# Reordering the prologue of a two-layer cross-attention kernel: loads from two queues, keys before queries, weight preparation moved to later slots

## The chip, the cores and the metric

The kernel runs on one NeuronCore of one Trainium2 chip. The metric is the device time of one launch in microseconds (us), as the median of several runs. The profile is one execution of the same program; its times count from the start of its span.

## What is computed

Four batches. Each has 256 queries (`x`) and 512 context rows (`ctx`), all 256 wide. Everything is kept close to float32: large products are made from a high and a low part of each operand.

```python
# layer 0, per batch
z = layer_norm(x, ln1_w, ln1_b)
q = z @ q_w + q_b;  k = ctx @ k_w + k_b;  v = ctx @ v_w + v_b     # 16 heads of 16
p = softmax(where(mask, q k^T / 4, -max))                          # 256 x 512 for each head
h = (p v) @ cproj_w + cproj_b + x
h = h + gelu(layer_norm(h, ln2_w, ln2_b) @ fc_w + fc_b) @ proj_w + proj_b
# layer 1, per batch
p1 = softmax((h w_q^T)(ctx w_k^T)^T / 16)
out = h + alpha * ((p1 (ctx w_v^T)) w_o^T)
```

## The kernel before, in words

Every engine runs its own program, written out by hand: a `prologue`, then `iteration(0)` to `iteration(3)`, then an `epilogue`. Engines meet only through semaphores, and each queue executes strictly in program order. SP issues nearly all transfers.

**Slots.** The attention of a batch is 16 heads in 4 groups of 4 heads, each group 8 tiles (a head's 128 queries by 512 keys). A slot handles one tile: `max_tile` multiplies `q_stack` by `k_stack` into `s1` (L546), VectorE takes the row maximum (`take_max`, L1284), `split_max` cuts the maxima into three bfloat16 parts, `max_rows` (L553) and `rows` (L977) write them into `q_stack`, `exp_tile` multiplies again, transposed and with the maxima subtracted (L563), ScalarE takes the exponential (L986), and `pv` multiplies by the values (L573). Maxima are one group ahead of exponentials. Slots are numbered 0 to 31 within a batch; iteration `b` runs slots 7 to 31 of batch `b` and 0 to 6 of batch `b+1`, and beside them, at slot numbers from the tables `PRE_AT` and `EARLY_AT`, the projections `pre(b+1, n)` of the next batch. `EARLY_AT` serves batch 1. Iterations 1 to 3 also carry the rest of the layers (`post`) of the batch before, which iteration 0 does not have. In its place iteration 0 prepares late weights: `PREP_AT` (TensorE, ScalarE) and `PREP_LOW_AT` (VectorE) give the slots of the steps WA, WT, CB, WO, WC, WF0, WF1, WP0, WP1 (L816 to L842 on TensorE).

**Stacks.** To reach float32 accuracy in bfloat16 products, a batch's queries `qp` and keys `kp` are cut into three parts (high, middle, low), and `stack_heads(b, c)` copies them, for the 8 heads of half `c`, into `q_stack` and `k_stack`: six transfers of 64 KB for the queries (L419), one mask row (L421), six transfers of 128 KB for the keys (L427). Before the change the queries go first. All 13 must land before half `c`'s first `max_tile`. For a later batch a half may be overwritten only once the exponentials that read it are through:

```python
await_alone(sp, s2_full, NS * (b - 1) + SLOTS * (2 * c + 2))
```

so `stack_heads(1, 0)` starts when slot 15 of batch 0 has been multiplied, and must land before slot 24, whose `max_tile` belongs to batch 1. `stack_heads(1, 1)` starts after slot 31.

**Parts.** The high part is written by ScalarE, the rest `qf - high` by GpSimd (`query_rest`, `key_rest`, L1627, L1635), the middle part by ScalarE, the low part by GpSimd (`query_low`, `key_low`, L1631, L1639). There is one buffer `kf` for both key halves.

**Prologue before.** SP loads `xz` (x of batch 0), `cx` (its context), `raw_q`, six rows of small vectors, two bias rows, `raw_k`, the mask and `raw_v`. TensorE transposes context and normalised x (`pre` with `U_CT`, `U_ZT`), then makes the vector columns (L854), a bias product (L859), turns the two bias rows into columns (L865), then `U_Q` (query product), `U_K`, `U_K+1` (key products), `U_V`, the 8 maxima of group 0, `U_V+1`, `max_rows` and slots 0 to 6. Products wait for low parts of weights that ScalarE and VectorE make. SP then issues the selector rows (L445), `stack_heads(0, 0)`, the loads of batch 1 (`load_pre(1)`: `xz`, mask, `cx`), `stack_heads(0, 1)`, and the late weights (L450 to L456).

The functions that the diff touches, with the line numbers of the profile:

Of the kernel before, what the change touches and what calls it, by code (L numbers as in the profile page):

```python
# [26 lines left out]
F32 = mybir.dt.float32  # L27
# [7 lines left out]
P = 128  # L35
B, LQ, D = 4, 256, 256
LK = 512
# [30 lines left out]

LN1_AT = 7
# [10 lines left out]
EARLY_AT = {7: U_CT, 8: U_CT + 1, 9: U_ZT, 10: U_Q, 14: U_K, 22: U_K + 1}  # L80
# [5 lines left out]
PREP_AT = {8: "WA", 10: "WT", 12: "CB", 13: "WO", 14: "WC", 16: "WF0", 18: "WF1", 24: "WP0", 26: "WP1",  # L86
           38: "END"}
PREP_LOW_AT = {11: "WT", 12: "WA", 13: "CB", 14: "WO", 15: "WC", 22: "WF0", 23: "WF1", 28: "WP1", 30: "WP0"}
# [36 lines left out]
def build(nc, x, ctx, mask, ln1_w, ln1_b, q_w, q_b, k_w, k_b, v_w, v_b, cproj_w, cproj_b, ln2_w, ln2_b,  # L125
          fc_w, fc_b, proj_w, proj_b, l1_q, l1_k, l1_v, l1_o, alpha, out):
    with ExitStack() as stack:
# [31 lines left out]
        bk = sb("bk", [P, DC])  # L159
        bf = sb("bf", [P, FC])  # L160
# [35 lines left out]
        qk_rows = oT[0:1, 0:2, :]  # L196
        qk_perm = oT[0:1, 2:4, :]
# [53 lines left out]
        l1_in, wf_in, wp_in = sem("l1_in"), sem("wf_in"), sem("wp_in")  # L251
# [53 lines left out]

        def pre_bank(b, n):

            if isinstance(b, int) and b == 0:
                return (pre_ps[:], post_ps[:, 0, :], post_ps[:, 1, :])[n % 3]
            return pre_ps[:]  # L310
# [86 lines left out]
        def _(sp):  # L397
# [11 lines left out]
            def stack_heads(b, c):  # L409

                heads = slice(c * HC, (c + 1) * HC)

                await_alone(sp, s2_full, NS * (b - 1) + SLOTS * (2 * c + 2))

                made = ((pre_free, PRE_USES * b + U_Q + 1), (qm_done, b + 1), (q_parts, b + 1))
                for part, (sem_, n) in enumerate(made):
                    await_alone(sp, sem_, n)
                    for i in [i for i, p in enumerate(TERMS_Q) if p == part]:
                        sp.dma_start(q_stack[i * HD:(i + 1) * HD, heads, :], qp[:, part, c, :]).then_inc(stacked[c], 16)  # L419
                await_alone(sp, row_done, b + 1)  # L420
                sp.dma_start(k_stack[ROW_MASK:ROW_MASK + 1, heads, :],  # L421
                             mask_row[0:1, :].unsqueeze(1).to_broadcast([1, HC, LK])).then_inc(stacked[c], 16)
                made = ((kh_done, 2 * b + c + 1), (km_done, 2 * b + c + 1), (k_parts, 2 * b + c + 1))
                for part, (sem_, n) in enumerate(made):
                    await_alone(sp, sem_, n)
                    for i in [i for i, p in enumerate(TERMS_K) if p == part]:
                        sp.dma_start(k_stack[i * HD:(i + 1) * HD, heads, :], kp[:, part, c, :]).then_inc(stacked[c], 16)  # L427

            def prologue():
                sp.dma_start(xz[:], x[0].rearrange("(p t) d -> p t d", t=TQ)).then_inc(x_in, 16)  # L430
                sp.dma_start(cx[:], ctx[0].rearrange("(p k) d -> p k d", k=TK)).then_inc(cx_in, 16)
                sp.dma_start(raw_q, q_w.rearrange("(c p) n -> p c n", p=P)).then_inc(wq_in, 16)
                row = 0
                for v in (ln1_w, ln1_b, v_b, ln2_w, ln2_b, fc_b):
                    n = v.shape[0] // P
                    sp.dma_start(vec_rows[row:row + n, :], v.rearrange("(r p) -> r p", p=P)).then_inc(vec_in, 16)
                    row += n
                for i, v in enumerate((q_b, k_b)):
                    sp.dma_start(qk_rows[:, i, :], v.rearrange("(o n) -> o n", o=1)).then_inc(bias_in, 16)
                sp.dma_start(raw_k, k_w.rearrange("(c p) n -> p c n", p=P)).then_inc(wk_in, 16)  # L440
                sp.dma_start(mask_u[:], mask[0:1, :].partition_broadcast(P)).then_inc(mask_in, 16)
                sp.dma_start(raw_v, v_w.rearrange("(c p) n -> p c n", p=P)).then_inc(wv_in, 16)
# [3 lines left out]
                stack_heads(0, 0)  # L446
                load_pre(1)
                stack_heads(0, 1)
                for t, w in zip(raw_l1, (l1_q, l1_k, l1_v, l1_o)):
                    sp.dma_start(t, w.rearrange("(c p) n -> p c n", p=P)).then_inc(l1_in, 16)  # L450
                sp.dma_start(raw_c, cproj_w.rearrange("(c p) n -> p c n", p=P)).then_inc(wc_in, 16)
# [31 lines left out]
        def _(pe):  # L483
# [25 lines left out]
            def pre(b, n):  # L509

                await_(pe, pre_free, PRE_USES * b + n if not (isinstance(b, int) and b == 0) else
                       n - 2 if n < U_Q else max(n - 2, U_ZT + 1))
# [297 lines left out]
            def prepare(step):  # L810

                if step == "WA":
                    pe.wait_ge(l1_in, 16 * 4)
                    for c in range(DC):
                        for k in range(DC):
                            mm = pe.matmul(post_ps[:, 0, c * D:(c + 1) * D], raw_l1[0][:, k, chunk(c)], raw_l1[1][:, k, :],  # L816
                                           start=k == 0, stop=k == DC - 1)
                    mm.then_inc(prep_ps, 1)
                elif step == "WT":
                    for c in range(DC):  # L820
                        for k in range(DC):
                            mm = pe.transpose(post_ps[:, 1, c * D + k * P:c * D + (k + 1) * P], raw_l1[3][:, k, chunk(c)], ident[:])
# [15 lines left out]
                elif step == "WO":  # L838
                    pe.wait_ge(w_lo, 4)
# [5 lines left out]
                elif step == "END":  # L845
                    pe.wait_ge(prep_done, 2)
                    pe.wait_ge(w_lo, 10)

            def prologue():
                pe.wait_ge(consts, 1)  # L850
                for n in range(U_CT, U_ZT + 1):
                    pre(0, n)
                pe.wait_ge(vec_in, 16 * 6)
                pe.transpose(s2[:, 0, 0:VECS], vec_rows[:], ident[0:VECS, 0:VECS]).then_inc(vec_ps, 1)  # L854

                pe.wait_ge(wq_in, 16)
                pe.wait_ge(vec_done, 2)
                for k in range(DC):
                    mm = pe.matmul(s2[0:1, 1, 0:D], vecs[:, V_LN1B + k:V_LN1B + k + 1], raw_q[:, k, :],  # L859
                                   start=k == 0, stop=k == DC - 1)  # L860
                mm.then_inc(bq_ps, 1)

                pe.wait_ge(bq_done, 2)
                for i in range(2 * DC):
                    mm = pe.matmul(s2[:, 1, D + i:D + i + 1], qk_perm[:, i // DC, chunk(i % DC)], ident[0:1, 0:1],  # L865
                                   start=True, stop=True)
                mm.then_inc(bq_ps, 1)
                pe.wait_ge(w_lo, 1)
                pre(0, U_Q)
                pe.wait_ge(w_lo, 2)  # L870
                pre(0, U_K)
                pre(0, U_K + 1)
                pe.wait_ge(w_lo, 3)
                pre(0, U_V)
                pe.wait_ge(sel_in, 16 * NG)
# [3 lines left out]
                max_rows(0, 0)  # L879
                for s in range(START):  # L880
# [56 lines left out]
        def _(act):  # L937
            def pre(b, n):
                if U_K <= n < U_V:
                    return  # L940
                act.wait_ge(pre_full, PRE_USES * b + n + 1)
# [4 lines left out]
                elif n == U_Q:  # L946
# [3 lines left out]
                    await_(act, q_parts, b)  # L950
                    for c in range(DC):
# [14 lines left out]
            def key_high(b, c):  # L966
                await_(act, stacked[c], 16 * STACK_DMAS * b)
                act.wait_ge(pre_free, PRE_USES * b + U_K + c + 1)
# [171 lines left out]
            def prepare(step):  # L1140
                if step == "WA":
                    act.wait_ge(prep_ps, 1)
                    act.activation(wa[0][:].rearrange("p c n -> p (c n)"), post_ps[:, 0, :], ACT.Copy, scale=L1_SCALE)\
                       .then_inc(w_hi, 1)
                elif step == "WO":
                    act.wait_ge(prep_ps, 4)
# [14 lines left out]
            def prologue():  # L1161
                for n in range(U_CT, U_ZT + 1):
                    pre(0, n)

# [5 lines left out]
                act.wait_ge(wk_in, 16)  # L1170
                for k in range(DC):
                    a = act.activation(parts_of(wk[0][:, k, :]), by_head(raw_k[:, k, :]), ACT.Copy)
# [604 lines left out]
```

## Time and profile before

| | |
|---|---|
| median of 3 runs | 336.18 us (334.94 to 336.44) |
| profiled execution, its own time | 335.6 us |
| its span | 333.8 us |
| TensorE matmul busy | 276.5 us, 83% |
| VectorE busy | 218.8 us, 66% |
| ScalarE busy | 189.9 us, 57% |
| GpSimd busy | 90.4 us, 27% |
| mean granted TensorE clock | 0.938 |
| moved by transfers | 21.59 MB |

In the rows below, PE is TensorE, PEld its weight load, DVE VectorE, ACT ScalarE, POOL GpSimd, SPq the issue of a transfer on SP. L numbers are lines of the kernel before. Busy shares are means over stages that have different limits, so the stage that changes has to be read by itself.

### The profile page before, as it was taken

To read this page: it belongs to the slowest core of one execution; us is meant where nothing else is said; L and a number is where in the kernel's file an instruction comes from. 1 tells how busy PE (TensorE), PEld (TensorE's weight loads), DVE (VectorE), ACT (ScalarE), POOL (GpSimd) and SP (SyncE) were. 2 spreads that over 40 slices of the span, in tenths; PEclk is the share of its full clock that TensorE was granted. 3 is DMA by queue.
4 is the path that set the end of the run, shared out by engine and by line. 5 is a ranking of instruction groups with operands and counts; after the bars stand their busy time and mean duration, and the time that the engine had idled before them with its cause. 6 is when DMAs were issued, how large, how long until landed. Compare 5 with 4: busy or idle time off the path is not lost.

```text
span 333.8 us, 5436 instructions
## 1 busy us (share of the span) xinstructions
PE 276.5 (83%) x2065; PEld 199.4 (60%) x2065; DVE 218.8 (66%) x430; ACT 189.9 (57%) x352; POOL 90.4 (27%) x87
## 2 busy tenths in 40 slices
PE   3670978987779897999898979998989997859895
PEld 3460426853226575866585758665956776658784
DVE  4550787377485967886758778867378664454854
ACT  3542084369565569596645695966466697315612
POOL 2143000212200138742002387440010354033300
PEclk9995599779589999999999999999999999978999
DMA  5129996007418202900443029004530000000000
GB/s 186 24 59 138 169 264 211 2 21 115 111 31 112 97 0 66 178 5 0 95 50 128 1 57 119 3 0 93 54 127 0 2 2 0 2 1 0 2 31 31
DMA packets 21489, 21.59 MB, mean 65 GB/s; under 512 B 2388, under 2 KB 18856, under 8 KB 21464
## 3 DMA queue, kind: packets, MB, share of 16 engines
q1 hardware_dynamic: 20168, 18.11, 28.8%
q10 hardware_dynamic: 1296, 3.15, 2.6%
q8 instruction: 16, 0.26, 0.3%
q14 instruction: 9, 0.07, 0.1%
HBM read 10.50 MB, written 1.05 MB: 35 GB/s over the span
## 4 chain that ended last, share of the span: by engine, by line
PE 46%; DVE 24%; ACT 12%; issue 5%; DMA 5%; SPq 4%; POOL 4%; ACTq 0%; DVEq 0%
DVE neg_max L1284 8%; PE post_ps L501 8%; PE om L573 6%; PE pre_ps L488 6%; PE s L546 5%; PE post_ps L505 4%; PE s L563 4%; DMA k_stack<-kp 3%; SPq L419 2%; ACT q_stack L977 2%; SPq L427 2%; PE s L501 2%; DVE ft L1367 1%; ACT probs L986 1%; PE post_ps L835 1%
## 5 line engine op out<-in xcount | busy, mean ns | idle before, releaser
L1284 DVE TENSOR_REDUCE neg_max<-s 128x1 f32<-128x512 f32 x128 | 83.4, 683 | 26.7 <-PE s L546 25.8
L986 ACT ACTIVATE probs<-s 128x512 f32<-128x512 f32 x128 | 75.5, 599 | 28.0 <-PE s L563 27.5
L546 PE MATMUL s<-k_stack,q_stack 97*128 97x512 bf16 x128 | 49.7, 414 | 21.5 <-DMA k_stack<-kp 14.9
L563 PE MATMUL s<-q_stack,k_stack 109*128 109x256 bf16 x256 | 50.6, 281 | 2.5 <-ACT q_stack L977 1.7
L546 PEld LDWEIGHTS s<-k_stack,q_stack 97*128 97x128 bf16 x128 | 12.4, 99 | 47.2 <-DVE neg_max L1284 21.8
L573 PE MATMUL om<-probs,vals 128*17 128x256 f32 x512 | 35.4, 397 | 0.0
L563 PEld LDWEIGHTS s<-q_stack,k_stack 109*128 109x128 bf16 x256 | 20.9, 101 | 16.6 <-ACT q_stack L977 3.6
L1615 POOL TENSOR_TENSOR ln<-ln,minus_half 128x2 f32<-128x2 f32 x8 | 5.6, 703 | 86.9 <-DVE ln L1248 86.9
L977 ACT ACTIVATE q_stack<-om 13x1024 bf16<-13x1024 bf16 x16 | 16.3, 1017 | 13.7 <-PE om L553 13.3
L573 PEld LDWEIGHTS om<-probs,vals 128*17 128x17 f32 x512 | 12.1, 99 | 14.0 <-issue 7.3
L1310 DVE TENSOR_TENSOR y_l<-post_ps,y_h 128x512 fp32r<-128x512 f32 x12 | 8.3, 689 | 16.3 <-ACT y_h L1000 16.3
L1367 DVE SCALAR_TENSOR_TENSOR ft<-ft,fx 128x512 f32<-128x512 f32 x9 | 12.0, 1331 | 7.2 <-POOL ft L1670 7.2
L1000 ACT ACTIVATE y_h<-post_ps 128x512 fp32r<-128x512 f32 x12 | 7.0, 595 | 17.0 <-PE post_ps L505 13.7
L1675 POOL TENSOR_TENSOR y_l<-fx,y_h 128x512 fp32r<-128x512 f32 x9 | 11.5, 1282 | 14.9 <-ACT y_h L1039 14.9
L501 PE MATMUL post_ps<-aT_h,wf_h 128*128 128x256 f32 x48 | 13.7, 319 | 0.0
L501 PE MATMUL post_ps<-wp_h,y_h 128*128 128x256 f32 x48 | 13.6, 314 | 0.0
L1670 POOL TENSOR_TENSOR ft<-fx 128x512 f32<-128x512 f32 x9 | 9.4, 1041 | 15.7 <-ACT fx L1013 15.7
L1635 POOL TENSOR_TENSOR kf<-kf,kp 128x512 f32<-128x512 f32 x8 | 9.3, 1161 | 15.2 <-ACT kp L969 15.2
L1657 POOL TENSOR_TENSOR h<-h,cb 128x512 f32<-128x512 f32 x3 | 3.8, 1271 | 32.2 <-DMA h<-in_x_dram 32.2
L1639 POOL TENSOR_TENSOR kp<-kf,kp 128x512 bf16<-128x512 f32 x8 | 10.2, 1272 | 7.0 <-ACT kp L973 7.0
L501 PE MATMUL post_ps<-wp_l,y_h 128*128 128x256 f32 x48 | 12.0, 283 | 0.0
L501 PE MATMUL post_ps<-aT_h,wf_l 128*128 128x256 f32 x48 | 12.0, 282 | 0.0
(315 smaller groups left out, 715.1 us busy)
## 6 DMA issues: line engine op xcount, KB each, us to landing
k_stack<-kp SPq DMA_DIRECT2D x48, 128.0 KB
q_stack<-qp SPq DMA_DIRECT2D x48, 64.0 KB
cx<-in_ctx_dram SPq DMA_DIRECT2D x4, 512.0 KB, 6.0
pcx<-in_ctx_dram ACTq DMA_DIRECT2D x3, 512.0 KB, 3.6
xz<-in_x_dram SPq DMA_DIRECT2D x5, 256.0 KB, 5.7
raw_late<-in_L_xattn_fc_w_dram SPq DMA_DIRECT2D x1, 1024.0 KB, 12.3
raw_late<-in_L_xattn_proj_w_dram SPq DMA_DIRECT2D x1, 1024.0 KB, 12.1
h<-in_x_dram ACTq DMA_DIRECT2D x3, 256.0 KB, 2.6
```

The lines of the kernel that those rows point to most:

```text
L488: mm = pe.matmul(o, wi(w[a], k), vi(v[c], k), start=start and k == 0 and i == 0, stop=stop and k == n - 1 and i == 2)
L501: pe.matmul(o, wi(w[a], k), vi(v[c], k), start=start and i == k == a == c == 0, stop=False)
L505: mm = pe.matmul(o, wi(w[late[0]], k), vi(v[late[1]], k), start=False, stop=stop and i == len(terms) - 1 and k == n - 1)
L546: pe.matmul(s1[:, s % 2, :], q_stack[0:ROW_MAX, hd, chunk(t)], k_stack[0:ROW_MAX, hd, :], start=True, stop=True).then_inc(s1_full, 1)
L563: mm = pe.matmul(s2[:, s % 2, i * LQ:(i + 1) * LQ], k_stack[:, hd, chunk(k)], q_stack[:, hd, :], start=True, stop=True)
L573: mm = pe.matmul(om[32 * j:32 * j + VW, 0:LQ], vals[:, k, g * GH + j, :], probs[:, g % 2, j, k, :], start=k == 0, stop=k == TK - 1)
L977: act.activation(q_stack[ROW_MASK:ROWS, g * GH:(g + 1) * GH, :], om_rows[ROW_MASK:ROWS, :].unsqueeze(1).to_broadcast([ROWS - ROW_MASK, GH, ...
L986: act.activation(probs[:, g % 2, s // 2, k:k + 2, :], s2[:, s % 2, :].rearrange("p (k n) -> p k n", k=2), ACT.Exp).then_inc(s2_free, 1)
L1284: dve.tensor_reduce(neg_max[:, g % 2, s % 2, s // 2:s // 2 + 1], s1[:, s % 2, :], AX.X, ALU.max, negate=True).then_inc(s1_free, 1)
L1367: dve.scalar_tensor_tensor(f, f, 1.0 / GELU_CUBIC, fx[i % 3], ALU.add, ALU.mult).then_inc(cube, 1)
L1639: pool.tensor_tensor(kp[:, 2, c, :], kf[:], kp[:, 1, c, :], ALU.subtract).then_inc(k_parts, 1)
L1675: pool.tensor_tensor(lo, fx[i % 3], hi.bitcast(F32), ALU.subtract).then_inc(y_split, 1)
```

## The change

SP and ScalarE both issue the first loads. The bias rows are no longer turned into columns by TensorE: four transfers write them as columns of 4-byte elements (`bk`, `qb`). The first key product stands ahead of the query product (`FIRST_ORDER`); the high part of the key weights is made by VectorE, its low part by GpSimd. The parts of the queries and of the first key half are cut on VectorE in place of GpSimd. `stack_heads(0, 0)` copies keys first. WA moves from iteration 0 into the prologue; the other preparation steps move to slots 16 and later. Selector rows, three late weights and `stack_heads(0, 1)` are reordered around the loads of batch 1, and `q_stack`'s memset is cut in two.

```diff
+FIRST_ORDER = (U_CT, U_CT + 1, U_ZT, U_K, U_Q, U_K + 1, U_V, U_V + 1)
-EARLY_AT = {7: U_CT, 8: U_CT + 1, 9: U_ZT, 10: U_Q, 14: U_K, 22: U_K + 1}
+EARLY_AT = {7: 0, 8: 1, 9: 2, 11: 3, 14: 4, 22: 5}
-PREP_AT = {8: "WA", 10: "WT", 12: "CB", 13: "WO", 14: "WC", 16: "WF0", 18: "WF1", 24: "WP0", 26: "WP1", 38: "END"}
-PREP_LOW_AT = {11: "WT", 12: "WA", 13: "CB", 14: "WO", 15: "WC", 22: "WF0", 23: "WF1", 28: "WP1", 30: "WP0"}
+PREP_AT = {16: "WT", 18: "WO", 19: "WC", 21: "CB", 22: "WF0", 24: "WF1", 28: "WP0", 30: "WP1", 38: "END"}
+PREP_LOW_AT = {17: "WT", 19: "WO", 21: "WC", 22: "CB", 24: "WF0", 26: "WF1", 31: "WP0", 36: "WP1"}

 # SP, stack_heads
+                if b == 0 and c == 0:
+                    keys()
+                    queries()
+                else:
+                    queries()
+                    keys()
 # SP, prologue, after xz and cx
-                (raw_q, six vector rows, two bias rows, raw_k, mask_u, raw_v, in this order)
+                for dst, v in ((bk, k_b), (qb, q_b)):
+                    for c in range(DC):
+                        sp.dma_start(dst[:, c:c + 1], v[chunk(c)].rearrange("(h d) -> d h", h=HC).unsqueeze(2),
+                                     allow_slow_non_contiguous=True).then_inc(bias_in, 16)
+                for i, w in ((0, l1_q), (1, l1_k)):
+                    sp.dma_start(raw_l1[i], w.rearrange("(p c) n -> p c n", c=DC)).then_inc(wa_in, 16)
+                stack_heads(0, 0)
                 sp.wait_ge(consts, 2)
                 for g in range(NG):
                     sp.dma_start(k_stack[ROW_MAX:ROWS, g * GH:(g + 1) * GH, :], sel[:]).then_inc(sel_in, 16)
-                stack_heads(0, 0)
+                for i, w in ((2, l1_v), (3, l1_o)):
+                    sp.dma_start(raw_l1[i], w.rearrange("(c p) n -> p c n", p=P)).then_inc(wo_in, 16)
+                sp.dma_start(raw_c, cproj_w.rearrange("(c p) n -> p c n", p=P)).then_inc(wc_in, 16)
+                stack_heads(0, 1)
                 load_pre(1)
-                stack_heads(0, 1)
-                (the four l1 weights and raw_c)
                 (raw_f, cb, pb, alpha_c, raw_p as before)
 # TensorE, prologue
+                vec_rows transposed first, then U_CT, U_CT + 1, U_ZT
+                bias product (4 matmuls of 128 columns), pre(0, U_K),
+                2 one-column matmuls for the bias product alone, pre(0, U_Q), pre(0, U_K + 1),
+                prepare("WA"), pre(0, U_V), 8 max_tile, pre(0, U_V + 1), max_rows
+                pe.wait_ge(sel_in, 16 * NG)      # now after max_rows, was ahead of the first max_tile
 # ScalarE, prologue
+                issues six vector rows, raw_k, raw_q, mask_u, raw_v; then
+                pre(0, U_CT); wq high; pre(0, U_CT + 1); pre(0, U_ZT); qk_row copy; wv high;
+                key_high(0, 0); key_middle(0, 0); pre(0, U_Q); query_middle(0); sel;
+                key_high(0, 1); key_middle(0, 1); prepare("WA"); pre(0, U_V); rows(0, 0); ...
 # VectorE, prologue
+                memset of half of q_stack; norm_stats; vecs; lnq; norm_apply; wk high; lows of U_CT, U_CT + 1;
+                wq low; low of U_ZT; take_mask; pre(0, U_K); bq (2 steps); key_rest(0, 0); wv low;
+                key_low(0, 0); query_rest(0); memset om; query_low(0); memset of the other half of q_stack;
+                pre(0, U_K + 1); memset vals; 8 take_max; split_max; prepare("WA")
 # GpSimd, prologue
+                wk low; mask_row_of(0); h; key_rest(0, 1); key_low(0, 1)
```

Lines with a sign and no code in them give in words the order that the new code has.

## Rows read from the trace of the kernel before

**Rows 1.** The chain that ended last, in order of time, prologue (start, length, what):

```profile
15.13 2.88 PE pre_ps L488 x12
...
27.56 5.73 DMA k_stack<-kp
```

**Rows 2.** SP's issues in order of time (start, length, engine, line, operation, tiles, count):

```profile
13.87 3.19 SPq L445 DMA_DIRECT2D k_stack<-fx  x4
...
24.37 3.79 SPq L427 DMA_DIRECT2D k_stack<-kp  x6
28.20 0.59 SPq L401 DMA_DIRECT2D xz<-in_x_dram  x1
...
72.34 3.77 SPq L419 DMA_DIRECT2D q_stack<-qp  x6
...
76.90 3.79 SPq L427 DMA_DIRECT2D k_stack<-kp  x6
```

**Rows 3.** The same chain in iteration 0:

```profile
51.97 1.73 PE post_ps L816 x8
...
57.89 0.44 PE post_ps L822 x4
...
60.30 0.86 PE post_ps L830 x4
61.16 4.46 PE post_ps L835 x32
...
66.49 3.41 PE post_ps L842 x8
...
80.09 5.74 DMA k_stack<-kp
```

**Rows 4.** Busy us by stretch: length, PE, PEld, DVE, ACT, POOL; granted clock, DMA share, GB/s:

```profile
52.00:72.30 20.30, 20.30 (x135) 15.90 (x134) 10.67 (x20) 8.60 (x18) 2.89 (x3) 0.83 0.17 52
72.30:81.50 9.20, 7.71 (x64) 3.38 (x62) 6.93 (x15) 8.39 (x15) 2.33 (x2) 1.00 0.55 98
...
96.20:110.10 13.90, 12.30 (x94) 7.18 (x92) 8.50 (x21) 8.46 (x15) 0.69 (x1) 0.88 0.58 87
28.00:30.00 2.00, 0.00 (x0) 0.00 (x0) 0.00 (x0) 1.11 (x2) 1.26 (x2) 0.50 1.16 119
32.00:34.00 2.00, 0.57 (x2) 0.14 (x2) 0.00 (x0) 0.00 (x0) 0.00 (x0) 0.50 1.02 268
...
98.00:100.00 2.00, 2.00 (x15) 0.73 (x19) 1.24 (x2) 0.73 (x2) 0.00 (x0) 0.50 0.32 83
```

**Rows 5.** The same view, one stretch inside the step CB:

```profile
61.00:62.00 1.00, 1.00 (x11) 1.00 (x9) 0.02 (x1) 0.00 (x0) 0.30 (x1) 1.00 0.00 0
```

**Rows 6.** Timeline (start, length, engine, line, operation, tiles, count, idle time before), prologue:

```profile
6.84 1.06 PE L517 MATMUL post_ps<-ident,xz 128*128 128x128 f32 x4
...
9.70 1.86 PE L859 MATMUL s<-probs,vecs 128*1 128x256 f32 x4 [1.57 <-DVE lnq L1431]
...
18.82 0.84 ACT L954 ACTIVATE qp<-pre_ps,bq 128x256 bf16<-128x256 f32 x2
...
20.14 0.75 DVE L1279 SCALAR_TENSOR_TENSOR kf<-post_ps,bk,mask_f 128x512 f32<-128x512 f32 x1
...
20.81 0.68 DVE L1383 TENSOR_TENSOR wv_l<-probs,wv_h 128x512 fp32r<-128x512 f32 x1
...
23.97 0.63 ACT L973 ACTIVATE kp<-kf 128x512 bf16<-128x512 f32 x1 [1.88 <-POOL kf L1635]
...
24.68 1.15 POOL L1639 TENSOR_TENSOR kp<-kf,kp 128x512 bf16<-128x512 f32 x1 [0.74 <-ACT kp L973]
```

**Rows 7.** Timeline, iteration 0: batch 1's first context transposes; a low part of weights:

```profile
48.16 0.61 PE L522 MATMUL pre_ps<-ident,cx 128*128 128x128 f32 x4
...
83.00 1.28 DVE L1408 SCALAR_TENSOR_TENSOR wf_l<-raw_late,vecs,wf_h 128x1024 fp32r<-128x1024 f32 x1
```

**Rows 8.** The page's DMA queues: packets, MB, share of 16 engines:

```profile
q1 hardware_dynamic: 20168, 18.11, 28.8%
```

More of the change, by code:

```diff
@@ L304, in bank_of, with pre_place, pre_use @@
             return POST_BANK[n]
+        def pre_place(b, n):
+            return FIRST_ORDER.index(n) if b == 0 else n
+        def pre_use(b, n):
+            return PRE_USES * b + pre_place(b, n) + 1
         def pre_bank(b, n):
-            if isinstance(b, int) and b == 0:
-                return (pre_ps[:], post_ps[:, 0, :], post_ps[:, 1, :])[n % 3]
+            if b == 0:
+                return (pre_ps[:], post_ps[:, 0, :], post_ps[:, 1, :])[pre_place(b, n) % 3]
             return pre_ps[:]
@@ L413, in stack_heads @@
                 await_alone(sp, s2_full, NS * (b - 1) + SLOTS * (2 * c + 2))
[L415 to L427, printed above, removed]
+                def queries():
+                    made = ((pre_free, pre_use(b, U_Q)), (qm_done, b + 1), (q_parts, b + 1))
+                    for part, (sem_, n) in enumerate(made):
+                        await_alone(sp, sem_, n)
+                        for i in [i for i, p in enumerate(TERMS_Q) if p == part]:
+                            sp.dma_start(q_stack[i * HD:(i + 1) * HD, heads, :], qp[:, part, c, :]).then_inc(stacked[c], 16)
@@ new lines, in keys @@
+                def keys():
+                    await_alone(sp, row_done, b + 1)
+                    sp.dma_start(k_stack[ROW_MASK:ROW_MASK + 1, heads, :],
+                                 mask_row[0:1, :].unsqueeze(1).to_broadcast([1, HC, LK])).then_inc(stacked[c], 16)
+                    made = ((kh_done, 2 * b + c + 1), (km_done, 2 * b + c + 1), (k_parts, 2 * b + c + 1))
+                    for part, (sem_, n) in enumerate(made):
+                        await_alone(sp, sem_, n)
+                        for i in [i for i, p in enumerate(TERMS_K) if p == part]:
+                            sp.dma_start(k_stack[i * HD:(i + 1) * HD, heads, :], kp[:, part, c, :]).then_inc(stacked[c], 16)
@@ L509, in pre @@
             def pre(b, n):
-                await_(pe, pre_free, PRE_USES * b + n if not (isinstance(b, int) and b == 0) else
-                       n - 2 if n < U_Q else max(n - 2, U_ZT + 1))
+                at = pre_place(b, n)
+                await_(pe, pre_free, PRE_USES * b + n if b > 0 else max(at - 2, DC if n == U_K else U_ZT + 1) if n > U_ZT else at - 2)
                 if n == U_ZT:
@@ L1161, in prologue @@
             def prologue():
-                for n in range(U_CT, U_ZT + 1):
-                    pre(0, n)
+                row = 0
+                for v in (ln1_w, ln1_b, v_b, ln2_w, ln2_b, fc_b):
+                    n = v.shape[0] // P
+                    act.dma_start(vec_rows[row:row + n, :], v.rearrange("(r p) -> r p", p=P)).then_inc(vec_in, 16)
+                    row += n
+                act.dma_start(raw_k, k_w.rearrange("(c p) n -> p c n", p=P)).then_inc(wk_in, 16)
+                act.dma_start(raw_q, q_w.rearrange("(c p) n -> p c n", p=P)).then_inc(wq_in, 16)
+                act.dma_start(mask_u[:], mask[0:1, :].partition_broadcast(P)).then_inc(mask_in, 16)
+                act.dma_start(raw_v, v_w.rearrange("(c p) n -> p c n", p=P)).then_inc(wv_in, 16)
+                pre(0, U_CT)
                 act.wait_ge(wq_in, 16)
@@ L1701, in prologue @@
                 rstd(ln1, ln1_step, 0, rstd1)
+                pool.wait_ge(wk_hi, 1)
+                for k in range(DC):
+                    i = pool.tensor_tensor(parts_of(wk[1][:, k, :]), by_head(raw_k[:, k, :]),
+                                           parts_of(wk[0][:, k, :]).bitcast(F32), ALU.subtract)
+                i.then_inc(wk_lo, 1)
+                mask_row_of(0)
                 pool.wait_ge(vec_done, 1)
@@ L1705, in prologue @@
                     .then_inc(prep_step, 1)
-                mask_row_of(0)
-                query_rest(0)
-                query_low(0)
-                for c in range(DC):
-                    key_rest(0, c)
-                    key_low(0, c)
+                key_rest(0, 1)
+                key_low(0, 1)
             def tail(step):
```

180 lines of the change are left out of this document (94 added, 86 removed).

## The prediction, made before the changed kernel ran

> **What bounds the kernel now.** I read the page first (busy shares, the 40 slices), then the chain that ended last in order of time, then SP's issues, the timelines and the busy time by stretch. TensorE is busy 83% of the span, and the chain goes through the same steps in iterations 1 and 2. The change does not touch them, so it can only move their start. The stage that matters is the prologue with iteration 0.
>
> In the prologue the chain ends in a transfer: the last key transfer is issued at 27.56 and lands at 33.29 [rows 1], and only then can the first `max_tile` run. SP's six key issues start at 24.37, so the keys take 8.92 us from first issue to landing; for batch 1 they take 76.90 to 85.83, 8.93 us [rows 2, 3]. That is the transfer engines at their limit, not SP: while keys move, the DMA share is 1.16 at 119 GB/s. While queries move it is 0.32 at 83 GB/s, paced by the issues. Loads from memory reach 268 GB/s [rows 4]. The queries stand ahead of the keys, so the slow part starts last.
>
> In iteration 0 the chain is TensorE. From 51.97 to 72.3 it is busy all 20.3 us [rows 4], and five preparation pieces stand in it: 1.73 + 0.44 + 0.86 + 4.46 + 3.41 = 10.9 us [rows 3]. Then slot 15 frees `stack_heads(1, 0)`, which runs from 72.34 [rows 2] to 85.83 [rows 3], 13.5 us. The work of slots 16 to 23 needs only 9.2 us of it [rows 4]; TensorE then waits. So there are two delays in series: the first stacks, and 10.9 us of preparation ahead of a transfer chain that has 4.3 us to spare.
>
> **Step 1, the first stacks.** TensorE finishes the transposes of x at 7.9 [rows 6], as now: the vector transpose ahead of them is short and x and the context come by the same two issues. The bias product costs 1.86 [rows 6], to 9.8. The key weights' low part on GpSimd must be there by then: two instructions of 256 columns, together about the 1.15 us of one of 512 columns [rows 6], after a VectorE copy that I bound by 0.68 [rows 6]. That ends near 9, so it is hidden; if the columns come strided and both double, it is 1 us late. The first key product is six matmuls of 512 columns, as much as twelve of 256, which took 2.88 with their tail [rows 1]; I take 2.7, to 12.5. VectorE evicts in 0.75, ScalarE makes the high part in 0.63 [rows 6]: first key issue at 14.0 in place of 24.37. The middle and low parts (0.68 on VectorE, 0.63, 0.68 [rows 6]) are ready before SP, at 0.63 an issue, wants them. Keys land at 14.0 + 8.9 = 22.9.
>
> The queries now come behind. Their product ends at about 15.7, two times 0.84 on ScalarE [rows 6] takes it to 17.3, and rest, middle, low (0.68 + 0.63 + 0.68) to 19.4, so SP's twelve issues run from 14.0 to 21.6 with almost no hole. The 384 KB of queries wait behind the keys and must drain after 22.9. Their own limit is not in the trace. At the loads' 268 GB/s they take 1.4 us; at the keys' 119 they take 3.2; if they pass beside the keys, nothing. Queries at 0.32 share were far from saturated, so I take the first end, 1.3: stacks at 24.2, **9.1 us earlier** than 33.29 (bounds 7.1 and 10.4).
>
> WA and the value product stay hidden: after the queries' product TensorE has the second key product (2.7), WA (1.73 to 3.41 [rows 3]) and values (2.7), which is 7.1 to 8.8 us after 15.7, at most 24.5. Here the cover is nearly used up. VectorE's half memsets lie before x arrives and after the last low part. ScalarE issues ten transfers before its first copy, which it cannot start before 6.2 anyway. The selector rows are needed only at the first exponential, 9 us later.
>
> The bias columns are four transfers of 128 elements of 4 bytes. They must land by 12.5, when the first key product is evicted, and behind VectorE's wait stand the queries' bias, all key and query parts and so both stacks. The queue's mean packet occupies an engine for 0.288 x 16 x 333.8 / 20168 = 0.076 us [rows 8]. With 512 packets over 16 engines that is 2.4 us after an issue before 4, landing well before 9: hidden, with 4 us to spare. The Trainium skill, "DMA: Bandwidth & Descriptors", Rules for kernel authors, says that a strided last dimension becomes one descriptor per element, which is the 512 packets counted here; no run so far shows such a transfer. By that rule alone the sum does not move, but it is the rule that speaks most against the change (see the last rival).
>
> **Step 2, batch 1's loads come later.** SP's order is now stacks (to 21.6), selector rows 3.2 [rows 2], three weights at 0.6 each (the issue of a load [rows 2]) to 26.6, queries of half 1 with mask row 4.5, keys from 31.2, landing at 40.1, then the loads of batch 1. Their 832 KB drain at 268 GB/s in 3.1 us, some of it beside the last keys: context in place at 43.0. TensorE wants it at 48.16 - 9.1 = 39.1 [rows 7] and stands still; behind it wait slot 7's exponential and the second half's maxima. Transposes, the high and low copy and the second transposes (0.61 + 0.63 + 0.68 + 0.61 [rows 6, 7]) bring it to 45.6, where it stood at 51.97: the gain is **6.4**, so 2.7 are given back. Bounds: nothing given back (now a norm and a copy stand there too), or 4.7 if the loads come 2 us later still. The Trainium skill, same page, Issuing engines are not separate DMA queues, says that two issuing engines save only issue time, since the same 16 engines move the data. The trace agrees in that 1.16 is reached from SP's queue alone.
>
> **Step 3, slots 8 to 15 without preparation.** 20.3 - 10.9 = 9.4 us of TensorE remain. ScalarE was busy 8.6 in this stretch and VectorE 10.7 [rows 4], part of it preparation. Such a stretch has waits: 9.4 is the lower bound, the 13.9 us of slots 32 to 38 with both value products [rows 4] the upper; I take 11.2. Slot 15 is done at 45.6 + 11.2 = 56.8, against 72.3.
>
> **Step 4, slots 16 to 23 with preparation.** 9.2 + 0.44 (WT) + 1.73 (WO, eight matmuls like WA's, at the upper clock) + 0.86 + 3.5 (CB) = 15.7 us. CB's 32 one-column matmuls took 4.46; at granted clock 1.00 eleven went in a us [rows 5], so 2.9 to 4.46, and I take 3.5. The stretch cannot be shorter than the stack chain, 13.5, nor, all at the lower clock, longer than 9.2 + 9.2 = 18.4. Now TensorE ends last, not the transfer. Slot 24 starts at 56.8 + 15.7 = 72.5 in place of 85.9: **13.4 earlier**.
>
> **Step 5, the rest of iteration 0.** A second fc_w low part (1.28 [rows 7]), its high part and one proj_w part now fall into slots 24 to 36. VectorE had waits there, so I take 1.8 in all (0 to 3.5). Left: 13.4 - 1.8 = **11.6 us**. From there everything shifts as a block: `EARLY_AT` differs from before by one slot for the query product.
>
> **Sum.** Against the profiled execution: 335.6 - 11.6 = 324.0. The median of the runs is 0.6 above that execution, so I put the forecast at 324.5.
>
> **Rivals.**
> - *The transfer engines take more back.* Queries drain at the keys' 119 GB/s (2.0 later) and batch 1's loads come 2 us later still: 328.5. For it: the stacks of half 1, selectors and weights crowd the same 14 us. Against it: queries were cheap. Chance 0.18.
> - *Preparation costs its full price later.* Slots 16 to 23 take 18.4 and the rest 3.5: 324.5 + 2.7 + 1.7 = 328.9. For it: during CB and WO the clock granted in the stretch was 0.83 [rows 4]. Against it: TensorE is no longer left idle after slot 23, which is where the level also falls now. Chance 0.14.
> - *More than forecast.* TensorE, busier from 5 to 20 us, gets the upper clock (2.4 GHz) early, which halves the first key product; the loads are on time and slots 16 to 23 fit the 13.5: 324.5 - 1.3 - 2.7 - 2.2 = 318.3. Chance 0.12.
> - *No effect.* Another wait (the stacks of half 1 before slot 8) takes the whole gain: they would have to land at 49 and not 40, which nothing in the sum suggests. 336. Chance 0.03.
> - *Slower: the bias columns.* If the 512 packets pass one after another through a single engine, they take 512 x 0.076 = 39 us and land at 43, 30 later than 12.5: about 354. It decides from a landing at 24.1, 11.6 behind the need. The one descriptor per element of the skill's page would be its cause. Against it: a 16-wide outer dimension should spread. Chance 0.04.
>
> **How the numbers follow.** The forecast (gain 8.5 to 15) has 0.49. Between 318 and 330 lie the forecast, the first two rivals and most of the third, some 0.85 in all with their overlaps. A change of 0.5% (1.7 us) is about what this measurement can tell from none. Faster: 0.49 + 0.18 + 0.14 + 0.12 = 0.93; same 0.03; slower 0.04.
>
> **What would show it.** First key issue near 14 and landing near 23; first `max_tile` near 24 with the last query transfer as its releaser; batch 1's first context transposes released by its load near 43; slot 15 near 57; between slots 23 and 24 no wait on a key transfer; first step of iteration 1 some 11.6 earlier and the same distance from there to the end as before. It fails if the releaser of the first key eviction is a bias transfer, if slot 24 still waits for the stacks (then step 3 was shorter or longer than I think and the 13.5 rules), or if the distance from iteration 1's first step to the end changes.

## The result and the profile after

The changed kernel takes 322.9 us (median of 4 runs, 322.44 to 323.04) against 336.31 in the same comparison: a ratio of 0.9609, 95% interval 0.9575 to 0.9643. The profiled execution took 322.9 us with a span of 321.1, so 12.7 us of span are gone; 11.6 were forecast. Executions more than 1.5% above the fastest of the same kernel are left out of the medians and ratios of all runs below.

**Profile after.** The chain that ended last, in order of time (start, length, what), answers to [rows 1, 3]:

```profile
5.70 0.26 PE s L870
...
9.40 0.69 DVE cT_l L1301
10.09 1.37 DVE wq_l L1485 x4
...
12.53 0.76 DVE kf L1310
13.31 0.64 ACT kp L992
13.97 0.65 SPq L441
...
35.01 1.97 SPq L412
...
37.50 5.82 DMA cx<-in_ctx_dram
...
45.49 1.13 PE pre_ps L538 x4
...
61.68 1.73 PE post_ps L860 x8
...
65.81 0.87 PE post_ps L848 x4
66.68 3.46 PE post_ps L853 x32
```

From 13.97 on the chain is an unbroken row of SP's issues, and it ends in the load of batch 1's context, landed at 43.3. No maximum of group 0 stands in it, and it waits for no stack transfer of half 0 to land. SP's pace is not what ends this row, though: one issue in it takes 1.97 us, and where that slow issue falls behind the context's load (the run with the first maxima delayed, below), the load is issued at 36.33 in place of 37.50 and still lands only 0.2 us sooner. From 16 to 48 us the transfer engines are nearly always busy (DMA share 0.93 to 1.23 in stretches of 2 us), so it is a row of transfers that ends there. WO (L860) and CB (L848, L853) now stand after 58.

SP's issues in order of time, which answer to [rows 2]:

```profile
13.97 3.87 SPq L441 DMA_DIRECT2D k_stack<-kp  x6
17.88 3.83 SPq L431 DMA_DIRECT2D q_stack<-qp  x6
21.75 3.15 SPq L462 DMA_DIRECT2D k_stack<-fx  x4
...
31.18 3.78 SPq L441 DMA_DIRECT2D k_stack<-kp  x6
35.01 1.97 SPq L412 DMA_DIRECT2D xz<-in_x_dram  x1
...
58.12 4.80 SPq L431 DMA_DIRECT2D q_stack<-qp  x6
```

TensorE's timeline, which answers to [rows 6, 7]:

```profile
10.46 0.50 PE L504 MATMUL pre_ps<-cT_h,wk_h 128*128 128x512 f32 x1
10.80 0.40 PE L504 MATMUL pre_ps<-cT_l,wk_h 128*128 128x512 f32 x1
11.03 0.40 PE L504 MATMUL pre_ps<-cT_h,wk_l 128*128 128x512 f32 x1
...
26.09 1.01 PE L562 MATMUL s<-k_stack,q_stack 97*128 97x512 bf16 x2 [7.27 <-DMA q_stack<-qp]
...
40.44 0.32 PE L569 MATMUL om<-ident_b,max_cols 128*109 128x128 bf16 x2 [0.94 <-DVE max_cols L1347]
43.45 0.63 PE L538 MATMUL pre_ps<-ident,cx 128*128 128x128 f32 x4 [2.68 <-DMA cx<-in_ctx_dram]
...
72.88 1.06 PE L562 MATMUL s<-k_stack,q_stack 97*128 97x512 bf16 x2
```

The first maxima start at 26.1, 7.3 us ahead of before (33.42). TensorE then stands idle for 2.7 us, from 40.8 until the context has landed. At 72.88 the maximum of slot 24, batch 1's first, follows without any wait for a stack, where [rows 3] show the key transfer at its end. Busy time by stretch (length, the five engines, granted clock, DMA share, GB/s):

```profile
22.00:24.00 2.00, 0.00 (x0) 0.00 (x0) 0.05 (x1) 0.73 (x2) 1.15 (x1) 0.90 1.23 123
24.00:26.00 2.00, 0.00 (x0) 0.00 (x0) 0.00 (x0) 1.47 (x3) 1.15 (x1) 0.50 0.93 116
...
44.00:46.00 2.00, 1.73 (x8) 0.77 (x7) 1.26 (x3) 1.08 (x2) 0.00 (x0) 0.52 0.99 342
...
58.10:72.90 14.80, 14.45 (x113) 10.47 (x112) 9.11 (x20) 8.88 (x16) 2.74 (x3) 0.95 0.69 116
72.90:83.30 10.40, 8.98 (x60) 3.11 (x59) 8.70 (x15) 9.38 (x16) 2.56 (x2) 0.74 0.09 34
```

While the last keys and the queries drain, the engines move 116 to 123 GB/s, the rate that [rows 4] show for keys. The step that stood at 111.76 in iteration 1 (the first maximum beside the normalised attention output of batch 0, L1284) is at 99.08 as L1331, 12.7 earlier, and from there to the end of the span it is 222.0 us both times.

### The profile page after: what moved, and what is told of

Its sections match the earlier page's. It is cut to its first block, busy times and chain, and to the rows that moved or that the text cites. A ratio compares the mean times of both kernels' runs of the same rounds, so it can differ in the third digit from the quotient of the medians.

```text
span 321.1 us, 5439 instructions
## 1 busy us (share of the span) xinstructions
PE 272.4 (85%) x2065; PEld 195.5 (61%) x2065; DVE 219.6 (68%) x433; ACT 188.6 (59%) x351; POOL 87.7 (27%) x85
## 2 busy tenths in 40 slices
DMA packets 21805, 21.59 MB, mean 67 GB/s; under 512 B 2962, under 2 KB 18916, under 8 KB 21780
## 3 DMA queue, kind: packets, MB, share of 16 engines
HBM read 10.50 MB, written 1.05 MB: 36 GB/s over the span
## 4 chain that ended last, share of the span: by engine, by line
PE 44%; DVE 21%; ACT 15%; SPq 7%; issue 5%; POOL 4%; DMA 3%; ACTq 1%; DVEq 0%
PE post_ps L517 8%; PE om L589 7%; PE pre_ps L504 6%; DVE neg_max L1331 5%; PE s L562 4%; PE s L579 4%; PE post_ps L521 4%; ACT q_stack L1000 3%; ACT probs L1009 3%; SPq L431 2%; SPq L441 2%; PE s L517 2%; DMA cx<-in_ctx_dram 2%; DVE ft L1414 1%; DVE cT_l L1301 1%
## 5 line engine op out<-in xcount | busy, mean ns | idle before, releaser
L1331 DVE TENSOR_REDUCE neg_max<-s 128x1 f32<-128x512 f32 x128 | 83.2, 683 | 19.6 <-PE s L562 18.8
L589 PEld LDWEIGHTS om<-probs,vals 128*17 128x17 f32 x512 | 12.2, 100 | 14.5 <-issue 7.8
L1723 POOL TENSOR_TENSOR y_l<-fx,y_h 128x512 fp32r<-128x512 f32 x9 | 11.6, 1283 | 14.8 <-ACT y_h L1062 14.8
L1683 POOL TENSOR_TENSOR kf<-kf,kp 128x512 f32<-128x512 f32 x7 | 8.1, 1161 | 23.5 <-ACT kp L992 23.5
L517 PE MATMUL post_ps<-wp_h,y_h 128*128 128x256 f32 x48 | 13.5, 313 | 0.1
L1687 POOL TENSOR_TENSOR kp<-kf,kp 128x512 bf16<-128x512 f32 x7 | 9.2, 1321 | 3.8 <-ACT kp L996 3.8
```

The source lines that it names most:

```text
L517: pe.matmul(o, wi(w[a], k), vi(v[c], k), start=start and i == k == a == c == 0, stop=False)
L589: mm = pe.matmul(om[32 * j:32 * j + VW, 0:LQ], vals[:, k, g * GH + j, :], probs[:, g % 2, j, k, :], start=k == 0, stop=k == TK - 1)
L1331: dve.tensor_reduce(neg_max[:, g % 2, s % 2, s // 2:s // 2 + 1], s1[:, s % 2, :], AX.X, ALU.max, negate=True).then_inc(s1_free, 1)
L1723: pool.tensor_tensor(lo, fx[i % 3], hi.bitcast(F32), ALU.subtract).then_inc(y_split, 1)
```

## The experiments

Times are medians; a ratio is against the kernel before on the same chip, with its 95% interval. The changed kernel is at 0.9609. Where a text compares traces, each is one execution.

**Queries first in half 0's stacks.**

```diff
-                if b == 0 and c == 0:
-                    keys()
-                    queries()
-                else:
-                    queries()
-                    keys()
+                queries()
+                keys()
```

> The changed kernel, with half 0's stacks in the old order (queries, then keys). Theory A (SP's row of issues and then batch 1's context load set slot 7; the changed kernel shows that load landing at 43.3 and TensorE idle 2.7 us before it): the first query issue can't be ahead of 16.8, keys follow from 21.5, every later issue of SP is 3.6 us late, the load lands near 46.9, and the time rises by about 3.6 us to 326.5. Theory B (the first maxima set slot 7 and all after it): keys land near 30.4 in place of 26.0, so 4.3 us more, 327.2. If keys-first is worth nothing, 322.9.

326.88 us, ratio 0.9695 (0.9665 to 0.9725). The order of the copies is worth 4.0 us; against the two runs on its own chip that time like the changed kernel (323.19 and 322.51, below), 3.7 to 4.4. SP's first copy is at 17.53 in place of 13.97, the first maximum at 31.11 in place of 26.09:

```profile
31.11 1.01 PE L558 MATMUL s<-k_stack,q_stack 97*128 97x512 bf16 x2 [11.57 <-DMA k_stack<-kp]
...
48.14 0.69 PE L534 MATMUL pre_ps<-ident,cx 128*128 128x128 f32 x4 [2.60 <-DMA cx<-in_ctx_dram]
```

The context landed 4.7 us later (48.0; theory A had 46.9), more than SP's row was late (3.6). The rest fits the transfers: from 18 to 24 us the queries move at a DMA share of 0.26 to 0.38 here, while in the changed kernel the keys, and the queries queued behind them, keep the engines busy (1.13 to 1.23). The time rose by 4.0, between the two theories' 3.6 and 4.3; they lie too near each other here, and the third run parts them.

**Preparation early again.**

```diff
-PREP_AT = {16: "WT", 18: "WO", 19: "WC", 21: "CB", 22: "WF0", 24: "WF1", 28: "WP0", 30: "WP1", 38: "END"}
+PREP_AT = {10: "WT", 12: "WO", 13: "WC", 14: "CB", 16: "WF0", 18: "WF1", 24: "WP0", 26: "WP1", 38: "END"}
-PREP_LOW_AT = {17: "WT", 19: "WO", 21: "WC", 22: "CB", 24: "WF0", 26: "WF1", 31: "WP0", 36: "WP1"}
+PREP_LOW_AT = {11: "WT", 13: "WO", 14: "WC", 15: "CB", 22: "WF0", 23: "WF1", 28: "WP0", 30: "WP1"}
```

> The changed kernel, with the preparation steps (all but WA, which stays in the prologue) moved back ahead of slot 16: WT 10, WO 12, WC 13, CB 14. Theory A (preparation belongs beside the 13.5 us of batch 1's stack transfers): slot 15 some 6.5 us later, then slots 16 to 23 wait for the transfers, so slot 24 comes at 58.1 + 6.5 + 13.6 = 78.2 in place of 72.9; up to 1.3 us of it is won back in slots 24 to 36. Time 327 to 328. Rival: the slots before 16 stand still for loads anyway, so preparation fits there: under 324.5.

326.9 us, ratio 0.9701 (0.9665 to 0.9738): 4.0 us more, as theory A has it. Slot 15 frees the stacks at 63.66 in place of 58.12 (5.5 us later; 6.5 expected), and slot 24 waits for them again, at 77.0 and not the expected 78.2:

```profile
77.00 1.03 PE L562 MATMUL s<-k_stack,q_stack 97*128 97x512 bf16 x2 [2.96 <-DMA k_stack<-kp]
```

**The first maxima delayed.**

```diff
                 pe.wait_ge(bq_done, 3)
+                pe.wait_ge(sel_in, 16 * NG)
                 for s in range(SLOTS):
                     max_tile(0, 0, s)
...
                 pe.wait_ge(w_lo, 3)
-                pe.wait_ge(sel_in, 16 * NG)
```

> The changed kernel, with TensorE's wait for the selector rows back ahead of the first maximum, which makes the first maxima about 2 us later (28 in place of 26.1) and moves no transfer. Theory A (batch 1's context load at 43.3 sets slot 7): TensorE's idle time ahead of that load shrinks from 2.7 to about 0.7 and the time stays at 322.9, within 0.5. Theory B (the first maxima are on the path): 324.9.

323.19 us, ratio 0.9565 (0.9522 to 0.9608): no more than the changed kernel. The delay of the first maxima, 2.15 us, was real, and it did not pass on to the time:

```profile
28.24 1.01 PE L562 MATMUL s<-k_stack,q_stack 97*128 97x512 bf16 x2 [9.25 <-DMA k_stack<-fx]
...
43.29 0.63 PE L538 MATMUL pre_ps<-ident,cx 128*128 128x128 f32 x4 [0.18 <-DMA cx<-in_ctx_dram]
...
46.10 0.66 PE L538 MATMUL pre_ps<-ident,cx 128*128 128x128 f32 x4 [1.52 <-DVE cT_l L1301]
```

Theory B falls: in the changed kernel the first maxima are not on the path. But the room is smaller than TensorE's 2.7 us of idle time. The second transposes of the context start at 46.10 in place of 45.49, released by VectorE, and this run's chain goes through the first maxima again. VectorE works in the order of its program: maxima of the second group, norm of batch 1's `x`, low part of the context. That order stands between first maxima and second transposes in the kernel before too, as its chain shows:

```profile
34.05 0.70 DVE neg_max L1284
...
43.43 3.69 DVE neg_max L1284 x6
...
51.31 0.66 PE pre_ps L522 x4
```

From the first maximum (33.42) to the second transposes (51.31) it is 17.9 us there, and here again 17.9 (28.24 to 46.10). In the changed kernel this path would be ready at 44.0 (26.09 + 17.9, an estimate from these two traces), and the context lets it be 45.49. So some 1.5 us are free, not 2.7.

**The parts on GpSimd again.** Rest and low parts of the first key half and of the queries go back from VectorE to GpSimd.

```diff
 # VectorE, prologue
-                key_rest(0, 0)
                 low_weights(wv[1][:], raw_v, wv[0][:], 2)
-                key_low(0, 0)
-                query_rest(0)
                 dve.memset(om[:], 0.0).then_inc(post_free[0], 1)
-                query_low(0)
 # GpSimd, prologue
+                key_rest(0, 0)
+                key_low(0, 0)
+                query_rest(0)
+                query_low(0)
                 key_rest(0, 1)
```

> The changed kernel, with the rest and low parts of half 0's keys and of the queries cut on GpSimd again (1.16 us each in place of 0.69). Theory A: SP issues a transfer each 0.64 us and is never short of a part, since three high parts take 1.9 us and two middle parts 1.3: key low parts are needed at 17.2 and come at 17.0, query low parts are needed at 21.1 and come at 19.9. No change: 322.9 within 0.5. Rival: the parts hold SP up, and the time rises by 1 to 2 us.

322.51 us, ratio 0.9584 (0.955 to 0.9619): no change. SP's row is the same to 0.05 us:

```profile
13.98 3.89 SPq L441 DMA_DIRECT2D k_stack<-kp  x6
17.91 3.83 SPq L431 DMA_DIRECT2D q_stack<-qp  x6
```

The split on VectorE is worth nothing that can be measured.

**Three late weights behind batch 1's loads.**

```diff
-                for i, w in ((2, l1_v), (3, l1_o)):
-                    sp.dma_start(raw_l1[i], w.rearrange("(c p) n -> p c n", p=P)).then_inc(wo_in, 16)
-                sp.dma_start(raw_c, cproj_w.rearrange("(c p) n -> p c n", p=P)).then_inc(wc_in, 16)
                 stack_heads(0, 1)
                 load_pre(1)
+                (the same three loads)
```

> The changed kernel, with the loads of three late weights (w_v, w_o, cproj_w, 0.77 MB) issued after batch 1's loads in place of ahead of half 1's stacks. Theory A (the transfer engines are full from 16 to 48, and batch 1's context ends that row): 1.5 us of issues and 2.2 us of transfer leave the path, the context lands near 41.1 in place of 43.3, and the time falls by about 2 us to 320.9. Rival (prologue and preparation alone set the time): 322.9.

321.23 us, ratio 0.9555 (0.952 to 0.9589). The direction is theory A's, but the interval overlaps that of the changed kernel. In the profiled execution the whole row started 1.15 us late (queries at 19.03), the context let TensorE go at 42.94, and the span is 321.1:

```profile
27.33 1.01 PE L562 MATMUL s<-k_stack,q_stack 97*128 97x512 bf16 x2 [7.63 <-DMA q_stack<-qp]
...
45.48 1.12 PE L538 MATMUL pre_ps<-ident,cx 128*128 128x128 f32 x4 [1.25 <-DVE cT_l L1301]
```

Counted from its own first key issue the load landed some 1.5 us sooner, but the first maxima came 1.2 us later, and the second transposes follow them by 18.2 us: the path through VectorE ended last, and nothing was won there. Inconclusive for the time.

**Batch 1's loads ahead of half 1's stacks.**

```diff
-                stack_heads(0, 1)
                 load_pre(1)
+                stack_heads(0, 1)
```

> The changed kernel, with batch 1's loads issued ahead of half 1's stacks, as before the change. Theory A: the context is there long before slot 7, but half 1's stacks now end the same row of transfers, near 43.3, and slot 8 waits for them: only the time between a landed context and its second transposes is won, 1 to 2 us, 321 to 322. Theory A', the load alone was the trouble and stacks pass beside it: 319.5 to 320.5. If the old order was worse: over 323.5.

319.48 us, ratio 0.9516 (0.9474 to 0.9558). TensorE's timeline:

```profile
40.84 0.32 PE L569 MATMUL om<-ident_b,max_cols 128*109 128x128 bf16 x2 [0.94 <-DVE max_cols L1347]
40.99 0.60 PE L538 MATMUL pre_ps<-ident,cx 128*128 128x128 f32 x4
41.44 0.38 PE L579 MATMUL s<-q_stack,k_stack 109*128 109x256 bf16 x2
43.29 1.04 PE L562 MATMUL s<-k_stack,q_stack 97*128 97x512 bf16 x2 [1.47 <-DMA k_stack<-kp]
44.14 1.12 PE L538 MATMUL pre_ps<-ident,cx 128*128 128x128 f32 x4
```

The context no longer stops TensorE, and half 1's stacks do, at the same 43.3: the row of transfers ends when it ended before, whatever stands last in it. What is won in this stretch is that the second transposes come at 44.14 in place of 45.49. That is the mechanism of theory A; the time is nearer to A' (319.5 to 320.5) than to A's 321 to 322.

**Both.** The loads first and the three weights last.

> The changed kernel, with batch 1's loads ahead of half 1's stacks and the three late weights behind both. Theory A: the row of transfers that slots 7 and 8 need ends near 41.1, and the context is no longer its last piece: both gains, 3 to 4 us, 319 to 320. Rival: TensorE's own work in slots 0 to 7 (first maxima at 26, slot 7 at 40.8) now ends last and only 2 us are to be had, 321.

319.69 us, ratio 0.9526 (0.948 to 0.9573). The time lies in theory A's range, but it is no better than the loads first alone, so there is no second gain to add. Slot 15 is at 55.46, 1.1 ahead of the run above, but the total did not show it. No transfer stops TensorE around slots 7 and 8 any more:

```profile
43.67 1.12 PE L538 MATMUL pre_ps<-ident,cx 128*128 128x128 f32 x4 [0.79 <-DVE cT_l L1301]
```

The chain now goes through the first maxima, 17.6 us ahead of these transposes (26.11), and VectorE's work between, which is what the rival said.

**Late preparation on the kernel before.**

```diff
-PREP_AT = {8: "WA", 10: "WT", 12: "CB", 13: "WO", 14: "WC", 16: "WF0", 18: "WF1", 24: "WP0", 26: "WP1", 38: "END"}
+PREP_AT = {16: "WA", 18: "WT", 20: "CB", 21: "WO", 22: "WC", 23: "WF0", 25: "WF1", 28: "WP0", 30: "WP1", 38: "END"}
-PREP_LOW_AT = {11: "WT", 12: "WA", 13: "CB", 14: "WO", 15: "WC", 22: "WF0", 23: "WF1", 28: "WP1", 30: "WP0"}
+PREP_LOW_AT = {17: "WA", 19: "WT", 21: "CB", 22: "WO", 23: "WC", 25: "WF0", 27: "WF1", 31: "WP0", 36: "WP1"}
```

> The kernel before, with all preparation steps (WA too) moved to slots 16 to 30, the prologue left as it was. Theory A: slots 8 to 15 lose 10.9 us of TensorE and keep some waits, so slot 15 is done near 63; slots 16 to 23 then need 9.2 + about 9.5 = 18.7 against 13.6 for batch 1's stacks: slot 24 near 82 in place of 85.9, time 336.3 - 3.5 = 332.8. Rival: nothing is hidden that was not hidden before, 336; or preparation accounts for all of the changed kernel's gain, 323 to 325.

334.67 us, ratio 0.9962 (0.9926 to 0.9998): 1.3 us by the ratio, less than the 3.5 expected and only just clear of nothing. Slot 24 did come at 82.52 (82 expected), but then:

```profile
65.40:82.50 17.10, 16.95 (x120) 12.92 (x119) 8.62 (x19) 7.71 (x15) 2.32 (x2) 0.90 0.66 121
82.50:95.80 13.30, 9.98 (x62) 3.28 (x60) 10.03 (x17) 10.97 (x17) 2.31 (x2) 0.74 0.00 1
```

Slots 24 to 31 took 13.3 us (10.3 in the kernel before) and gave 3 of the 3.4 back in this execution: ScalarE is busy 11.0 of it and VectorE 10.0, and ScalarE makes four large high parts in the stretch (`wf_h` and `wp_h`, two each). The changed kernel has 10.4 us there with three, at the same granted clock of 0.74. The next run tests this.

**A fourth piece in slots 24 to 31 of the changed kernel.**

```diff
-PREP_AT = {16: "WT", 18: "WO", 19: "WC", 21: "CB", 22: "WF0", 24: "WF1", 28: "WP0", 30: "WP1", 38: "END"}
-PREP_LOW_AT = {17: "WT", 19: "WO", 21: "WC", 22: "CB", 24: "WF0", 26: "WF1", 31: "WP0", 36: "WP1"}
+PREP_AT = {16: "WT", 18: "WO", 19: "WC", 21: "CB", 24: "WF0", 25: "WF1", 28: "WP0", 30: "WP1", 38: "END"}
+PREP_LOW_AT = {17: "WT", 19: "WO", 21: "WC", 22: "CB", 25: "WF0", 27: "WF1", 31: "WP0", 36: "WP1"}
```

> The changed kernel, with the two fc_w steps moved from slots 22 and 24 to 24 and 25 (their low parts to 25 and 27). Theory C (from the run with late preparation on the kernel before: its slots 24 to 31 took 13.3 us with ScalarE busy 11.0, where the changed kernel takes 10.4 with 9.4): slots 24 to 31 are held by ScalarE and VectorE once a fourth high part falls into them; they stretch by 1 to 1.5 us, and the time rises as much, to 324. Theory A alone (only TensorE and the stack transfers count): 322.9, within 0.5.

324.7 us, ratio 0.9647 (0.9607 to 0.9686), 1.8 above the changed kernel's 322.9 and 2.9 above its run on the same chip (321.75, below). Slot 24 is at 73.16 (0.3 later), slot 31 frees the next stacks at 85.54 in place of 83.28: the stretch grew by 2.0.

```profile
73.20:85.50 12.30, 8.26 (x61) 3.08 (x60) 9.18 (x16) 10.78 (x17) 2.41 (x2) 0.86 0.11 40
```

TensorE is busy less than in the changed kernel's 10.4 us (8.26 against 8.98), and the granted clock is higher (0.86 against 0.74), so neither TensorE's work nor its clock makes the stretch longer. ScalarE is busy 10.8 of the 12.3 us. Theory C holds: from slot 24 on, the copies of the weights count, those on ScalarE above all, and not TensorE.

**The changed kernel and the loads first, side by side.** No edits beyond the ones shown.

> The changed kernel itself, on the same chip as its neighbours here, for comparison: 322.9. Theory D (the mean granted clock of an execution moves the time by up to 4 us, as the runs with 0.936 and with 0.961 suggest): single times spread from about 319.5 to 323.5 and follow the clock.

> The changed kernel with batch 1's loads ahead of half 1's stacks, once more, beside the changed kernel on one chip. Theory A: TensorE is not stopped ahead of slot 7, 1.5 to 3 us less than its neighbour, 320 to 321.4. If the gain seen before was only the clock of those executions: the same as its neighbour.

321.75 us, ratio 0.9573 (0.9534 to 0.9612), and 319.92 us, ratio 0.9522 (0.9485 to 0.956). Side by side the loads first are 1.8 us better than the changed kernel; against its first median, 322.9, the two runs with the loads first are 3.0 and 3.4 better. Their intervals lie below that of its first run (0.9575 to 0.9643) and overlap that of the run beside them, so a gain is likely and its size open. With the weights last or without, these are the best versions seen: 0.952 of the kernel before. Single times of the changed kernel lay between 320.1 and 322.9, the shortest at the highest clock, as theory D has it.

## Why the prediction was right, step by step

**Step 1 was right in its start and wrong in its end.** The first key copy was issued at 13.97 (14.0 forecast), but by luck in part, for the path to it was another. TensorE began late because its first instruction waited for the small vectors, issued on ScalarE and landed at 5.6, so the key product started at 10.46 and not 9.8; and it ran with a step of 0.23 us and not 0.45 for 512 columns, at the upper clock level, so it was done at 12.1 and not 12.5. That is one condition of the third rival come true, but the 1.3 us that the rival expected from it were not won: VectorE reached the eviction of the keys only at 12.53, having worked from 9.40 without a gap through the low parts of context, weights and `x` and the mask, which the sum left out. The mis-sized term is the drain of the queries, taken as 1.3 us: the first maximum came at 26.1 and not 24.3. The bound that the prediction set aside, 3.2 us at the keys' rate, is what the stretches from 22 to 26 show. The 268 GB/s behind the 1.3 was also no rate of loads alone: in that stretch (32 to 34) the last keys still moved until 33.29, and loads alone reach 342 to 410 GB/s (42 to 46 in the changed kernel). The same rival's other half, loads 2 us later still, did not come true.

**That miss cost nothing, because step 2 is the gate.** The sum took the context's landing from the row of issues and transfers and not from the first maxima, and that landing was 43.3 (43.0). The first rival therefore added 2 us too many: by the prediction's own sum, queries that drain 2 us later do not move the context. The delayed maxima show that about 1.5 us there are free; had the drain been 1.5 us longer still, it would have been the gate. Yet the sentence on step 1 as a gain of 9.1, of which 2.7 are given back, reads as if it carried the total. Measured at the second transposes, the first maxima came 7.3 us sooner, and the late context took back 1.5 of that (45.49 against 44.0). What the early key issue did was to start the row of transfers 5.7 us sooner (13.97 against 19.68) and to fill the engines from its start; queries-first takes back 4.0. The second transposes ended at 46.6 and not 45.6: 0.3 of it is the later landing, and about 0.45 that they ran at the lower clock level (1.13 us against 0.66), granted clock 0.52 in that stretch.

**Steps 3 and 4.** Slot 15 was done at 58.1 (56.8), 11.5 us after the transposes (11.2 taken). Slots 16 to 23 with preparation took 14.8 (15.7), with CB's small matmuls at 3.46 (3.5). Slot 24 came 13.0 earlier (13.4). The early preparation shows the mechanism: 4.0 us for moving four TensorE steps and the copies. One floor was higher than the 13.5 us taken: the first six issues of the stacks took 4.80 us here (3.77 before), and in two other executions slot 24, 14.4 to 14.5 us after the stacks were freed, did wait a moment for its keys. The changed kernel run again shows it (stacks freed at 58.42):

```profile
72.91 0.60 PE L562 MATMUL s<-k_stack,q_stack 97*128 97x512 bf16 x2 [0.27 <-DMA k_stack<-kp]
```

So TensorE's work and the stack transfers end within a few tenths of a microsecond of each other there, and by these traces less preparation in this stretch would win almost nothing; that was not tried.

**Step 5 was too high**: 1.8 taken, 0.3 measured (13.0 - 12.7). Slots 24 to 31 took 10.4 us against 10.3 before, with a third high part among them. The crowded slots show where the price jumps: three large high parts in these slots fit, the fourth costs about 2.

**How the parts add.** The new prologue with early preparation is worth 9.4 us (336.3 to 326.9), late preparation on the old prologue 1.3 (0.38% of 336.4), on the new one 4.0. They are more than additive, partly because the edits differ: in the changed kernel WA already sits in the prologue, whose TensorE had room (it stands idle from 18.8 to 26.1), so slots 16 to 24 have less to take. Of the 9.4 us of the new prologue the order of the copies accounts for 4.0. How the rest divides among the loads from two queues, the bias columns, keys ahead of queries on TensorE and WA's new place was not tried. The split between VectorE and GpSimd has no measurable part in it.

**The bias columns** were hidden as forecast: transfers of 128 elements landed 3.4 to 4.3 us after their issue (2.4 was the estimate), the last near 8.1, against a need at 12.5. Packets under 512 B rose from 2388 to 2962, which fits the 512 counted. What they do cost is SP: 0.65 us an issue, 2.6 in all, at a time when SP has nothing urgent to issue. They were not tried in another form.

What stays open: how much of the 1.8 to 3.4 us of the reordered loads comes from the order and how much from the clock of single executions, what makes one issue of SP take 1.6 to 2.0 us in these runs, and what sets the 120 GB/s of the copies into the stacks.

## What to carry to other kernels

Find the gate behind the gate: an early start at the head of an in-order issue queue shifts everything behind it, and the gain is read at the last transfer of that row, not at the first consumer. Then measure the room to the next gate on every engine: TensorE's idle time (2.7 us here) overstated it, since VectorE's program order left only 1.5. Fixed work belongs in the stretch whose end is set by a transfer chain, up to the engine that fills first there, which may be the one that makes the copies and not the one that multiplies. Bound a drain behind a saturated stream by that stream's rate, unless a row shows otherwise.

## What the runs showed that was not expected

Copies from one place of on-chip memory to another moved 116 to 123 GB/s in the changed kernel from 18 to 26 us, at a DMA share of 0.93 to 1.23, for the keys' rows of 1 KB and, once they queue, for the queries' rows of 512 B alike. Loads ran at 342 to 410 GB/s at a share of 0.99 to 1.05 (42 to 48 us).

Executions of one program differ by 2.9 to 4.6 us in most of these variants, and there the shorter ones have the higher mean granted clock: spans of 318.2 and 321.1 us at 0.951 and 0.945 (changed kernel, one chip), 315.1 and 319.7 at 0.961 and 0.941 (loads first, weights last). That is no law: in the kernel before, spans of 333.3 us stand at 0.932 and spans of 335.8 at 0.938. In the profiled execution of the changed kernel the granted level is 0.50 (the lower of the two, 1.2 GHz) from 24 to 32 us and near 0.5 again from 44 to 50, after TensorE had stood idle from 18.8 to 26.1 and from 40.8 to 43.5. Whether the clock or something that goes with it makes the difference was not tested. Differences under 1% between variants need many runs.
